# Attention block on one NeuronCore: softmax weights scaled by their own row inverses before the product with the values, in place of row sums on the matrix engine

## The reference, cut to what matters

```python
q, kv = ln(x), ln(ctx)
qp, kp, vp = q @ Wq.T + bq, kv @ Wk.T + bk, kv @ Wv.T + bv      # 16 heads of 32
scores = einsum('bhld,bhtd->bhlt', qh, kh) / sqrt(32)
bias   = -spatial_scale * dist(query_xy, token_xy) + spatial_offset
attn   = softmax(where(mask, scores + bias, -inf), axis=-1)
x = x + einsum('bhlt,bhtd->bhld', attn, vh).reshape(16, 256, 512) @ Wo.T + bo
h = gelu(ln(x) @ W1.T + b1)
x = x + h @ W2.T + b2
```

## Time and profile before

| | |
|---|---|
| median of 3 runs | 1309.01 us (1306.88 to 1309.49) |
| the profiled execution, its own time | 1308.17 us |
| its span on the core | 1306.4 us |
| TensorE matmuls busy | 1225.2 us, 10240 instructions |
| VectorE busy | 972.1 us |
| ScalarE busy | 793.2 us |
| GpSimd busy | 980.0 us |
| 16 slots (one batch) in the steady part | 72.08 us |
| mean granted clock of TensorE | 0.966 of full speed |

### The profile page before, as it was taken

The page is one execution under the profiler, slowest core; times in us unless marked ns, Lnnn a source line. Parts: engine busy times, 40 slices in busy tenths (PEclk is TensorE's granted clock), DMA queues, the critical chain, the costliest instruction groups (busy, mean ns, idle before and its releaser), DMA issues.

```text
span 1306.4 us, 27978 instructions
## 1 busy us (share of the span) xinstructions
PE 1225.2 (94%) x10240; PEld 834.5 (64%) x10240; DVE 972.1 (74%) x2203; ACT 793.2 (61%) x1323; POOL 980.0 (75%) x1158
## 2 busy tenths in 40 slices
PE   5688758999999999999999999999999999999998
PEld 5466335666767666666667676666667676766664
DVE  5588997778878787777788787877777886767321
ACT  4565756675656666576756666565767566665332
POOL 5476788788879787888889797888888896857321
PEclk9876778999999999999999999999999999999999
DMA  8458897797989888889979898988899897777534
GB/s 259 122 120 203 198 236 182 171 209 173 201 199 202 185 181 199 193 195 192 222 167 216 177 203 188 203 185 194 197 186 226 164 210 175 161 161 174 138 105 129
DMA packets 468201, 241.69 MB, mean 185 GB/s; under 512 B 383568, under 2 KB 408416, under 8 KB 468064
## 3 DMA queue, kind: packets, MB, share of 16 engines
q1 hardware_dynamic: 468064, 239.91, 80.9%
HBM read 109.66 MB, written 12.58 MB: 94 GB/s over the span
## 4 chain that ended last, share of the span: by engine, by line
PE 73%; ACT 11%; DVE 5%; issue 4%; POOL 3%; DMA 2%; SPq 1%; POOLq 0%; DVEq 0%; ACTq 0%
PE ps_down L605 21%; PE ps_up L590 21%; PE ps_qk L519 10%; PE ps_vo L543 6%; PE ps_vo L540 4%; PE ps_s L554 4%; PE ps_pv L568 4%; PE ps_pv L576 2%; ACT soft L705 2%; ACT L705 1%; ACT L721 1%; ACT L736 1%; DVE soft L964 1%; ACT ps_down L662 1%; ACT u L736 1%
## 5 line engine op out<-in xcount | busy, mean ns | idle before, releaser
L590 PE MATMUL ps_up<-hT,w 128*128 128x256 f16 x3072 | 378.8, 273 | 0.1
L605 PE MATMUL ps_down<-w,hid 128*128 128x512 f16 x1536 | 372.9, 379 | 0.5 <-DVE hid L1003 0.4
L705 ACT ACTIVATE soft<-soft,neg_max 128x256 f32<-128x256 f32 x512 | 232.8, 502 | 215.4 <-DVE neg_max L964 213.2
L590 PEld LDWEIGHTS ps_up<-hT,w 128*128 128x128 f16 x3072 | 301.4, 98 | 89.1 <-issue 0.6
L964 DVE CUSTOM_DVE_ANT_0 soft<-ps_s,soft,factor 128x256 f32<-128x256 f32 x512 | 226.1, 478 | 135.8 <-PE ps_s L554 135.4
L730 ACT ACTIVATE u<-ps_up,bias,up_scale 128x256 f32<-128x256 f32 x256 | 143.0, 559 | 171.4 <-PE ps_up L590 169.6
L1139 POOL TENSOR_SCALAR p_nat<-soft 128x512 f16<-128x512 f32 x256 | 187.9, 734 | 72.3 <-ACT soft L705 67.3
L605 PEld LDWEIGHTS ps_down<-w,hid 128*128 128x128 f16 x1536 | 148.5, 97 | 132.2 <-DMA w<-x_scratch 1.0
L1146 POOL TENSOR_SCALAR soft<-dist,scale_neg,offset 128x512 f32<-128x512 f32 x256 | 225.5, 881 | 3.5 <-DVE p_nat L970 3.5
L970 DVE SCALAR_TENSOR_TENSOR p_nat<-soft,p_nat 128x512 f16<-128x512 f32 x256 | 222.8, 871 | 0.5 <-POOL p_nat L1139 0.5
L1165 POOL TENSOR_SCALAR hid<-u,hid_scale 128x1024 f16<-128x1024 f32 x64 | 74.2, 1159 | 116.2 <-ACT u L736 116.2
(11 more groups left out here) (114 smaller groups left out, 1605.2 us busy)
## 6 DMA issues: line engine op xcount, KB each, us to landing
w<-x_scratch SPq DMA_DIRECT2D x256, 256.0 KB, 3.1
stack<-qk_parts SPq DMA_DIRECT2D x256, 96.0 KB
raw<-in_ctx SPq DMA_DIRECT2D x32, 256.0 KB, 3.8
raw<-in_x SPq DMA_DIRECT2D x32, 256.0 KB, 3.1
c_stage<-in_w SPq DMA_DIRECT2D x8, 1024.0 KB, 6.6
x<-in_x SPq DMA_DIRECT2D x32, 256.0 KB, 3.5
out<-x SPq DMA_DIRECT2D x32, 256.0 KB, 3.3
tok_rows<-in_tok_xy SPq DMA_DIRECT2D x16, 256.0 KB, 4.9
```

Of the source, the lines that this page charges most:

```text
L590: mm = e.matmul(ps_up[s % 2][:, 0:L], w_1_sb[:, wp, k, m * P:(m + 1) * P], hT[:, b % 2, :, xp * KT + k, :], start=(k, wp, xp) == (0, 0, 0) ...
L605: mm = e.matmul(ps_down[tt][:], hid[:, chunk % HID_RING, i, hp, tt * P:(tt + 1) * P], w_2_sb[:, s % W2_RING, wp, :], start=(m == 0 and (hp ...
L705: e.activation(soft[:, ring, lc, :], soft[:, ring, lc, :], ACT.Exp, scale=-1.0, bias=neg_max[:, ring, lc:lc + 1]).then_inc(s_exp)
```

## The change

1. `exps` now also adds up each row of exponentials (`accum_out` into `row_sum`), per half.
2. A new step `inverse(k)` on VectorE, in slot 2k+2, takes the row sums of two items, 128x4 numbers, and makes 2^14 over the sum (a reciprocal, then a multiplication), after it has waited for all four exponentials of both items.
3. `p_hi` and `p_lo` scale by this inverse instead of by 2^14. It differs between the two halves of an item, so each of the two steps is now two instructions of 128x256 with a per-partition factor instead of one of 128x512. They and the DMA transpose stand one slot later (2, 3 and 4), and so does `attend` (slot 9). On GpSimd `p_hi` now comes behind `bias_tile` in a slot.
4. The 16 matmuls with `ones` are gone from `attend`; so are the reciprocal and the multiplication of `attn_scale`.
5. The parts of the attention output are made straight from PSUM, scaled by 2^-14: `attn_hi` on ScalarE and `attn_lo` on VectorE, both in slot 4G+10. GpSimd has no part in it any more.
6. The ring of `soft` grows from 5 to 6.

```diff
@@ tensor_program, attend
-                gate.wait_ge(s_y, G)
+                gate.wait_ge(s_alo, G)
...
-                gate.wait_ge(s_id, ID_ONES)
-                sums_of = [(tc, pp) for tc in range(TC) for pp in (HI, LO)]
-                for n, (tc, pp) in enumerate(sums_of):
-                    for j in range(HPG):
-                        mm = e.matmul(ps_pv[32 * j:32 * j + 32, L:2 * L], ones[:], pT[:, (4 * G + j) % PT_RING, pp * LC * TC + tc:(pp + 1) * LC * TC:TC, :],
-                                      start=(n == 0), stop=(n == len(sums_of) - 1))
                 mm.then_inc(s_pv)
...
-                for G in due(slot, 8, GROUP, N_HG):
+                for G in due(slot, 9, GROUP, N_HG):
                     attend(G)
@@ scalar_program
             def exps(i):
                 ring = i % SOFT_RING
+                gate.wait_ge(s_one, (i - SOFT_RING) // 2 + 1)
                 for lc in range(LC):
                     gate.wait_ge(s_max, 2 * i + lc + 1)
-                    e.activation(soft[:, ring, lc, :], soft[:, ring, lc, :], ACT.Exp, scale=-1.0, bias=neg_max[:, ring, lc:lc + 1]).then_inc(s_exp)
+                    e.activation(soft[:, ring, lc, :], soft[:, ring, lc, :], ACT.Exp, scale=-1.0, bias=neg_max[:, ring, lc:lc + 1],
+                                 accum_out=row_sum[:, ring, lc:lc + 1]).then_inc(s_exp)
+            def attn_hi(G):
+                b, hg = divmod(G, HG)
+                gate.wait_ge(s_pv, G + 1)
+                gate.wait_ge(s_o, n_half(b - 2, 1))
+                e.activation(attnT[:, b % 2, HI, hg, :], ps_pv[:, 0:L], ACT.Copy, scale=1.0 / P_SCALE).then_inc(s_ahi)
...
+                for G in due(slot, 10, GROUP, N_HG):
+                    attn_hi(G)
                 for i in due(slot, 0, ITEM, N_ITEMS):
                     exps(i)
@@ vector_program
+            def inverse(k):
+                pair_of = slice(2 * k % SOFT_RING, 2 * k % SOFT_RING + 2)
+                gate.wait_ge(s_exp, 4 * k + 4)
+                gate.wait_ge(s_inv, k - SOFT_RING // 2 + 1)
+                e.reciprocal(row_one[:, pair_of, :], row_sum[:, pair_of, :]).then_inc(s_one)
+                gate.wait_ge(s_one, k + 1)
+                gate.wait_ge(s_plo, 2 * k - SOFT_RING + 2)
+                e.tensor_scalar(row_inv[:, pair_of, :], row_one[:, pair_of, :], P_SCALE, None, ALU.mult).then_inc(s_inv)
+
             def p_lo(i):
-                nat = i % NAT_RING
+                nat, ring = i % NAT_RING, i % SOFT_RING
                 gate.wait_ge(s_phi, i + 1)
-                e.scalar_tensor_tensor(out=p_nat[:, nat, LO, :, :], in0=soft[:, i % SOFT_RING, :, :], scalar=P_SCALE,
-                                       in1=p_nat[:, nat, HI, :, :], op0=ALU.mult, op1=ALU.subtract).then_inc(s_plo)
-
-            def attn_scale(G):
-                gate.wait_ge(s_pv, G + 1)
-                e.reciprocal(attn_inv[:], ps_pv[:, L:2 * L]).then_inc(s_ainv)
...
-                e.tensor_tensor(attn_y[:], ps_pv[:, 0:L], attn_inv[:], ALU.mult).then_inc(s_y)
+                for lc in range(LC):
+                    mine = e.scalar_tensor_tensor(out=p_nat[:, nat, LO, lc, :], in0=soft[:, ring, lc, :], scalar=row_inv[:, ring, lc:lc + 1],
+                                                  in1=p_nat[:, nat, HI, lc, :], op0=ALU.mult, op1=ALU.subtract)
+                mine.then_inc(s_plo)
+
+            def attn_lo(G):
+                b, hg = divmod(G, HG)
+                gate.wait_ge(s_ahi, G + 1)
+                e.scalar_tensor_tensor(out=attnT[:, b % 2, LO, hg, :], in0=ps_pv[:, 0:L], scalar=1.0 / P_SCALE, in1=attnT[:, b % 2, HI, hg, :],
+                                       op0=ALU.mult, op1=ALU.subtract).then_inc(s_alo)
@@ gpsimd_program
             def p_hi(i):
-                gate.wait_ge(s_exp, 2 * i + 2)
+                nat, ring = i % NAT_RING, i % SOFT_RING
+                gate.wait_ge(s_inv, i // 2 + 1)
...
-                e.tensor_scalar(p_nat[:, i % NAT_RING, HI, :, :], soft[:, i % SOFT_RING, :, :], P_SCALE, 1.0, ALU.mult, ALU.mult).then_inc(s_phi)
+                for lc in range(LC):
+                    mine = e.tensor_scalar(p_nat[:, nat, HI, lc, :], soft[:, ring, lc, :], row_inv[:, ring, lc:lc + 1], 1.0, ALU.mult, ALU.mult)
+                mine.then_inc(s_phi)
-            def attn_hi(G):
...
-            def attn_lo(G):
```

More of the change, by code:

```diff
@@ L82, in sb @@
             return nc.alloc_sbuf_tensor_at(name, shape, dt, offset=off)
-        SOFT_RING, NAT_RING, PT_RING, STACK_RING, DIST_RING, X1_RING, U_RING, HID_RING, W2_RING = 5, 4, 6, 2, 2, 6, 2, 2, 3
+        SOFT_RING, NAT_RING, PT_RING, STACK_RING, DIST_RING, X1_RING, U_RING, HID_RING, W2_RING = 6, 4, 6, 2, 2, 6, 2, 2, 3
         CH, XT_RING = 4, 3
-        ones = sb("ones", [P, HD], F16)
         cols_sb = sb("cols", [P, cols.shape[1]], F32)
@@ L98, in build_block @@
         shift = sb("shift", [P, 6], F32)
+        row_sum = sb("row_sum", [P, SOFT_RING, LC], F32)
+        row_one = sb("row_one", [P, SOFT_RING, LC], F32)
+        row_inv = sb("row_inv", [P, SOFT_RING, LC], F32)
         sums = sb("sums", [P, 37], F32)
@@ L147, in build_block @@
         square_out = sb("square_out", [P, KT * D], F32, at["x1"])
-        mask_f32 = sb("mask_f32", [B, T], F32, at["attn_y"])
+        mask_f32 = sb("mask_f32", [B, T], F32, at["x1"] + (KT + 1) * D * 4 + 4 * T)
         sq = sb("sq", [P, LC, T], F32, at["x1_n"])
@@ L188, in build_block @@
         s_xy, s_sq, s_d2, s_dist, s_mrow = sem("s_xy"), sem("s_sq"), sem("s_d2"), sem("s_dist"), sem("s_mrow")
-        s_bias, s_score, s_max, s_exp, s_phi, s_plo = [
-            sem(n) for n in ("s_bias", "s_score", "s_max", "s_exp", "s_phi", "s_plo")]
-        s_pt, s_pv, s_ainv, s_y, s_ahi, s_alo = sems("s_pt", PT_RING), sem("s_pv"), sem("s_ainv"), sem("s_y"), sem("s_ahi"), sem("s_alo")
+        s_bias, s_score, s_max, s_exp, s_one, s_inv, s_phi, s_plo = [
+            sem(n) for n in ("s_bias", "s_score", "s_max", "s_exp", "s_one", "s_inv", "s_phi", "s_plo")]
+        s_pt, s_pv, s_ahi, s_alo = sems("s_pt", PT_RING), sem("s_pv"), sem("s_ahi"), sem("s_alo")
         s_res, s_xbo, s_o, s_x1, s_xb2 = sems("s_res", X1_RING), sem("s_xbo"), sem("s_o"), sem("s_x1"), sem("s_xb2")
@@ L436, in sync_program @@
                     stack_copies(G)
-                for i in due(slot, 3, ITEM, N_ITEMS):
+                for i in due(slot, 4, ITEM, N_ITEMS):
                     p_turn(i)
@@ L1016, in vector_program @@
                     score_max(i)
+                for k in due(slot, 2, 2, N_ITEMS // 2):
+                    inverse(k)
                 for b, n in at_tile(slot, (-30, -29, -17, -17), (-27, -26, -23, -22)):
@@ L1055, in vector_program @@
                         mlp_out(2 * b + tt)
-                for i in due(slot, 2, ITEM, N_ITEMS):
+                for i in due(slot, 3, ITEM, N_ITEMS):
                     p_lo(i)
@@ L1060, in vector_program @@
                         qk_lo(G, which)
-                for G in due(slot, 9, GROUP, N_HG):
-                    attn_scale(G)
+                for G in due(slot, 10, GROUP, N_HG):
+                    attn_lo(G)
                 for chunk in due(slot, UP + CH + 1, CH, B * N_CHUNKS):
@@ L1178, in add_b_2 @@
                 e.tensor_tensor(tile, tile, b_2_sb[:], ALU.add).then_inc(s_xb2)
-            e.memset(ones[:], 1.0).then_inc(s_id)
             e.memset(one[:], 1.0).then_inc(s_id)
@@ L1187, in gpsimd_program @@
             for slot in range(FIRST_SLOT, LAST_SLOT + 1):
-                for i in due(slot, 1, ITEM, N_ITEMS):
-                    p_hi(i)
                 for w in range(N_W):
@@ L1205, in gpsimd_program @@
                     bias_tile(i)
-                for G in due(slot, 10, GROUP, N_HG):
-                    attn_hi(G)
-                    attn_lo(G)
+                for i in due(slot, 2, ITEM, N_ITEMS):
+                    p_hi(i)
                 for b in due(slot, -15, BATCH, B):
```

14 lines of the change are left out of this document (1 added, 13 removed).

## The result

The change runs in 1302.7 us (median of 7 runs, 1297.9 to 1304.4) against 1309.2 us before; the ratio is 0.994, with a 95% interval of 0.9921 to 0.9959. It is faster, by 6.5 us where 21 were forecast, and lies 0.7 us above the upper end of the forecast range, 1302. The profiled execution took 1303.1 us, and so belongs to the slower ones of the seven: what a single profile gives for a part of the run holds for that execution.

A forecast was written before the change was run, and what follows sets the result against it. TensorE was taken to bound each batch, except for one ScalarE window. Terms -26.1 + 3.7 + 1.3 + 0 = -21.1 us took the profiled 1308.2 to 1287.1, median 1288; range 1278 to 1302.

The forecast's parts named there:

- The matmuls with `ones`, -26.1 us: On TensorE's chain, removing the 1024 matmuls saves 26.1 us, at 0.44 us for each group of 16.
- The far end of 32 us: The same saving at 0.54 us a group, if the tenth at the switch to full-wide matmuls also went.
- The reads in the window, +3.7: ScalarE's row-sum reads lengthen its critical window by 0.28 us per pair over thirteen batches; ends +2.1 and +7.8.
- The cover of slot 2, +1.3 us: ScalarE's wait for `mlp_up` before the window shrinks by 1.17 us; 0.1 us a batch, upper end +5.6.
- the cover is just used up: Claim that losses of 0.28, 0.45 and 0.44 us equal ScalarE's 1.17 us wait for `mlp_up` in slot 2.
- one regular exception: Claim that TensorE bounds the batch except at its wait for `v_parts`, once a batch, where ScalarE's 8.84 us window binds.
- Start and end, 0: Before 222 us and from 1165 to 1201 us, gains and losses on VectorE, GpSimd and ScalarE nearly cancel: 0.
- The five us to each side: Uncertainty of 5 us either way put on the zero for the run's start and end.
- GpSimd and VectorE in the steady part: Both stay hidden by TensorE: GpSimd 61.8 us a batch with `p_hi` halves at 0.62, VectorE at most 56.
- The slower rival: GpSimd becomes the bound through `p_hi` halves at 0.75 us: +25 us, 1333; chance 0.14.
- ScalarE's window takes most of it: Rival: both ScalarE terms reach their upper ends, giving 1296, or 1302 with more critical table-load slots; chance 0.15.
- The clock rival: With less work in the start, TensorE is granted a lower clock for one more stretch: 1296; chance 0.08.

The follow-up runs named there:

- e4: The change with the 16 matmuls with `ones` of each group put back behind the 24 with the values, result unread; 1322.1 us.
- e7: The kernel before with row sums (`accum_out`) added to its `exps`, which nobody reads; 1313.9 us.
- e12: The kernel before with the square root `dist_sqrt` four slots later and nothing else; 1293.1 us.
- e8: The change with `attn_hi` ahead of `qk_hi` on ScalarE and the square root `dist_sqrt` four slots later; 1276.8 us.
- e5: The change without `accum_out` in `exps`, the row sums being a constant written once; 1293.5 us.
- e6: The change without `inverse(k)`: `p_hi` waits for its own exponentials, and both parts scale by a constant; 1291.7 us.
- e3: The change with `p_hi` and `p_lo` as one 128x512 instruction each, scaled by the first half's inverse; 1303.1 us.
- e9: The change with `inverse(k)` still issued but nobody waiting for it; `p_hi` and `p_lo` scale by a constant; 1297.9 us.
- e13: e8 with the multiplication of each inverse by 2^14 moved from VectorE to GpSimd, just ahead of `p_hi`; 1272.4 us.

## Why the prediction was right and wrong

*The matmuls with `ones`, -26.1 us: right.* The regular batch shows 0.435 to 0.44 us a group in four pairs of kernels: 72.26 (e4) and 72.26 (e7) against the change's 70.52, 71.32 (e12) against 69.57 (e8), 72.08 (before) against 70.33 (e5). The far end of 32 us is excluded: the tenth at the switch from quarter-wide to full matmuls stays. Before, the matmuls with `ones` start 0.66 us behind the first of the 24 with the values; in the change a full matmul follows the 24, and starts 0.77 us behind their first (645.28 to 646.05). The Trainium skill ("TensorEngine Tiling (Array Packing)", Key Properties) says that a change of tiling mode drains TensorE, and the trace agrees with these 0.11 us.

*The reads in the window, +3.7: the mechanism right, the size 0.19 a batch instead of 0.28.* The timeline of the change shows why: an exponential starts at 436.16 and the next at 436.65, 0.49 apart instead of 0.41, and the pair is 0.18 longer.

*The cover of slot 2, +1.3 us: the first step that failed.* The three terms were added up correctly to 1.17, and "the cover is just used up" then set this against the idle time of one batch, as if all had it. Only three of the twelve had, and eight had 0.3 us or less: ScalarE's wait for the `stack` DMAs differs from batch to batch, and with no cover each lateness comes through. The trace of before was enough to see it. An estimate from its twelve idle times: 1.17 us less each of them gives 8.7 us in all instead of 1.3; with what the parts really took (0.18 for the reads and 0.27 for `attn_hi`, and the forecast's 0.44) it is 6.2. Measured: the irregular batches cost 11.6 us where before they cost 2.4, +9.2 where +1.3 was taken and 5.6 was the upper end. Of this, 5.7 us are longer waits for `v_parts` and 3.4 a lower clock behind two of them (last section), for which the forecast had no term. Two batches of before already ran 0.3 and 0.6 us long in this way, with the chain off TensorE, so "one regular exception" was not all that the chain showed. That the change makes the DMAs themselves later is not borne out: `qk_hi` starts on average 1.93 us ahead of the end of `mlp_up` before and 1.40 in the change, and 0.44 of these 0.53 are `mlp_up` ending sooner.

*Start and end, 0: the second step that failed.* The end gained 3.3 us, some 2 of them the matmuls with `ones` (e4, which has them, has 148.2 there against 146.1), which the -26.1 holds already. The start lost 9.5. The sum said that "VectorE loses reciprocals" and that all "nearly cancel"; it set up no list for the stretch in which VectorE is busiest (102.6 of the 118 us up to 218). In that list 15.2 us go (the reciprocals and their multiplications), and 19.0 come in: `p_lo` +9.3, the inverse 6.8, `attn_lo` 2.9. That is 3.8 more, not 9.5: without the inverse 8.0 us come back (e6), while the larger halves of `p_lo` give next to nothing (e3). The five us to each side were a guess without a row.

*GpSimd and VectorE in the steady part: right.* GpSimd is busy 61.3 us in the 70 shown against 61.8 forecast for a batch; its halves took 0.66 us against 0.62, and VectorE 57.4 against 56. The slower rival never came near. `p_lo`'s halves took 0.59 instead of 0.47. e9 has as many halves beside each other on both engines, but a constant in place of the factor from memory:

```profile
L1156 POOL TENSOR_SCALAR p_nat<-soft 128x256 f16<-128x256 f32 x512 | 285.9, 574 | 1.7 <-DMA pT<-p_nat 1.2 <-ACT soft L699 0.5
...
L984 DVE SCALAR_TENSOR_TENSOR p_nat<-soft,p_nat 128x256 f16<-128x256 f32 x512 | 213.1, 456 | 0.0
```

They take 0.57 and 0.46. With the factor but the work in other places in time (e13) they take 0.59 and 0.56. So `p_lo`'s excess goes mostly with the factor, and GpSimd's at least in part with what runs beside it. The Trainium skill ("GPSIMD Engine Reference", Key points) names shared SBUF interfaces and Vector instructions with two SBUF inputs; by that rule the half would have moved from 0.62 towards 0.75. It went to 0.66, and no run here shows the rule by itself.

*The rivals.* "ScalarE's window takes most of it" (1296 to 1302, given 0.15) is what happened in the batches; the start then carried the time past it. The clock rival is not supported: e4 gives TensorE its work back and the start does not move. The granted clock up to 218 us is lower in the change (0.74, before 0.81), but it does not go with the start: in e3 it is 0.84 and the start 226.6, in e6 0.77 and the start 219.8.

In sum: 1308.2 - 22.7 (13 batches at 1.75) - 3.3 (end) + 2.3 (reads) + 9.2 (irregular) + 9.5 (start) = 1303.2, against 1303.1 of the profiled execution.

*Open.* The start is known by single profiles, and its parts do not add up: the inverse gives back 8.0, the reads 2.3, `attn_hi` first 2.5, which is more than 9.5 together. They may overlap; no run took them out jointly. Why the DMAs into `stack` land late in some batches and not in others was not tried. The profile of the change shows two forms: at 428.6 us a load of `w_2` ahead of them held SP's queue for 1.58 us (0.71 at 641 us, in a regular batch), and ahead of the two longest waits `qk_hi` could start only 4.05 and 3.60 us behind the last issue (1.82 in the batch at 658.09).

## What to carry to other kernels

Before adding work ahead of a critical stretch, read its cover (the idle time in front of it) in every batch and not in one; where a DMA comes before it, price the step by the spread. A unit that is 65% busy can still set the pace for 9 us in 70; look for the stretch where it runs without a gap, and move what has the longest slack (here one square root with its table load) out of it, since that can be worth more than the change itself. A prologue with its own bound needs its own list of instructions, and the sum of busy times does not price it: here the tiny ones of the inverse cost 6 to 8 us, and merging the larger halves gained 1.
